# Last stage of a fused attention and mixture-of-experts kernel: the scores' small products in one piece, the sums' small products in one piece, and the transposes of the sums ahead of the mask

## What is computed

```python
h = einsum('bhid,oi,od->bho', x, weighted_sum, weight)        # token mixing, image tokens only
h = concatenate([h, txt], axis=1)
h = h + attention(layernorm(h))      # 16 heads of 16, cosine scores over the 8 batch rows of a token
h = h + ffn(layernorm(h))

def ffn(x):                                                   # the last stage
    q = (rmsnorm(x) @ Wq + bq).reshape(b, t, 16, 16)
    k, v = split(((rmsnorm(x) @ Wdown + bdown) @ Wup + bup).reshape(b, t, 16, 32), 2, axis=-1)
    att = softmax(einsum('bthd,btgd->bthg', q, k) / sqrt(16)) # a token's 16 heads against each other
    x = x + (einsum('bthg,btgd->bthd', att, v).reshape(b, t, 256) @ Wo + bo)
    h2 = rmsnorm(x)
    gate = softmax(h2 @ Wg + bg)                              # 8 experts, all of them used
    return x + einsum('btd,edf,bte->btf', h2, We, gate)
```

## Time and profile before

| what | value |
|---|---|
| median of 3 runs | 841.62 us (840.92 to 843.73) |
| the profiled execution | 842.31 us, span in the profile 840.5 us |
| mean granted TensorE clock | 0.974 |
| PE busy | 777.3 us, 92% |
| PE weight loads busy | 516.1 us, 61% |
| DVE busy | 730.3 us, 87% |
| ACT busy | 335.5 us, 40% |
| POOL busy | 413.3 us, 49% |
| scores' small products (line 868) | 4736 records, 57.2 us |
| sums' small products (line 879) | 4736 records, 56.5 us |

### The profile page before, as it was taken

The page is one execution under the profiler, slowest core; times in us unless marked ns, Lnnn a source line. Parts: engine busy times, 40 slices in busy tenths (PEclk is TensorE's granted clock), DMA queues, the critical chain, the costliest instruction groups (busy, mean ns, idle before and its releaser), DMA issues.

```text
span 840.5 us, 48630 instructions
## 1 busy us (share of the span) xinstructions
PE 777.3 (92%) x20348; PEld 516.1 (61%) x20348; DVE 730.3 (87%) x1702; ACT 335.5 (40%) x874; POOL 413.3 (49%) x1158
## 2 busy tenths in 40 slices
PE   4999978998989899976899999999999999999998
PEld 3888755666666666654556666665666566666654
DVE  5799578899999999964789999999999999999997
ACT  4577333444444444422333333333333333333331
POOL 1331355566666666672445544554455545554321
PEclk9999998999999999975899999999999999999999
DMA  9985000000000000000000000000000000000000
GB/s 328 335 230 190 1 4 4 1 0 0 0 0 0 0 0 0 2 4 3 4 16 16 6 12 12 12 6 12 12 12 12 6 12 12 12 6 13 13 17 20
DMA packets 17062, 28.33 MB, mean 34 GB/s; under 512 B 3475, under 2 KB 12259, under 8 KB 17003
## 3 DMA queue, kind: packets, MB, share of 16 engines
q1 hardware_dynamic: 17002, 27.49, 10.1%
HBM read 22.64 MB, written 4.83 MB: 33 GB/s over the span
## 4 chain that ended last, share of the span: by engine, by line
PE 52%; DVE 1%; issue 1%; ACT 0%; POOL 0%; ACTq 0%
PE bank L197 12%; PE bank L199 10%; PE bank L198 10%; PE bank L868 6%; PE bank L879 6%; PE bank L895 2%; PE bank L933 2%; PE bank L886 2%; PE bank L939 1%; PE bank L919 1%; PE bank L920 1%; DVE sc L1041 0%; DVE smax L1038 0%; DVE acc L1026 0%; DVE res L1026 0%
## 5 line engine op out<-in xcount | busy, mean ns | idle before, releaser
L197 PE MATMUL bank<-we_h,h_t_h 128*128 128x512 f16 x296 | 113.0, 382 | 0.2
L199 PE MATMUL bank<-we_h,h_t_l 128*128 128x512 f16 x296 | 112.2, 379 | 0.0
L198 PE MATMUL bank<-we_l,h_t_h 128*128 128x512 f16 x296 | 112.2, 379 | 0.0
L1026 DVE SCALAR_TENSOR_TENSOR acc<-bank,gate,acc 128x256 f32<-128x256 f32 x222 | 105.4, 475 | 7.0 <-PE bank L199 2.5
L197 PE MATMUL bank<-tokw_h,x_t_h 128*128 128x256 f16 x256 | 70.8, 277 | 11.4 <-DVE x_t_l L643 11.4
L198 PE MATMUL bank<-tokw_l,x_t_h 128*128 128x256 f16 x256 | 70.7, 276 | 0.0
L199 PE MATMUL bank<-tokw_h,x_t_l 128*128 128x256 f16 x256 | 70.7, 276 | 0.0
L879 PEld LDWEIGHTS bank<-pr_t,v 32*32 32x32 f32 x4736 | 48.0, 105 | 33.6 <-issue 33.6
L466 POOL TENSOR_TENSOR rt<-rn 128x32 f32<-128x32 f32 x111 | 26.6, 240 | 80.9 <-DVE rn L441 75.1
L868 PEld LDWEIGHTS bank<-kv_t,fq_t 32*32 32x32 f32 x4736 | 48.8, 107 | 17.7 <-issue 17.7
L879 PE MATMUL bank<-pr_t,v 32*32 32x32 f32 x4736 | 56.5, 194 | 2.7 <-issue 2.6
(11 more groups left out here) (207 smaller groups left out, 2231.0 us busy)
## 6 DMA issues: line engine op xcount, KB each, us to landing
xbuf<-in_x SPq DMA_DIRECT2D x32, 512.0 KB, 5.4
out<-res SPq DMA_DIRECT2D x36, 128.0 KB
we_s<-in_we SPq DMA_DIRECT2D x4, 512.0 KB, 7.0
inw<-in_in_w SPq DMA_DIRECT2D x1, 768.0 KB, 11.3
wrep<-in_w_rep SPq DMA_DIRECT2D x1, 512.0 KB, 4.9
h_all<-in_txt SPq DMA_DIRECT2D x1, 512.0 KB
wst<-in_wst_in SPq DMA_DIRECT2D x1, 256.0 KB, 2.7
outw<-in_out_w SPq DMA_DIRECT2D x1, 256.0 KB, 11.1
```

The costliest lines, as they stand in the source:

```text
L197: nc.tensor.matmul(dst, a_h(c), b_h(c), start=start and c == 0, stop=False)
L198: nc.tensor.matmul(dst, a_h(c), b_l(c), start=False, stop=False)
L199: last = nc.tensor.matmul(dst, a_l(c), b_h(c), start=False, stop=stop and c == chunks - 1)
L1026: op = nc.vector.scalar_tensor_tensor(out=(res if e == E - 1 else acc)[:, :], in0=b_we[s % 2][:, k * D:(k + 1) * D], scalar=gate[p][:, e:e ...
```

## The change

PE's body in the last stage gets another order. No instruction of computation is added or removed, and the programs of the other engines stay as they are.

- The transposes of `on` come first in the body, ahead of the mask.
- The 16 score pieces follow the mask in one go; the semaphore `f_s` is set before the `q` product instead of after it.
- The 16 sum pieces are made in one go before expert step 2; `f_av` is set before expert step 2 instead of after it.

```diff
             def body(i, p):
-                if real(i, 0):
-                    pe.wait_ge(f_qt, i + 1)
-                    nc.tensor.matmul(b_s3[:, :], fm[:, 0:P], fm[:, P:], start=True, stop=True,
-                                     skip_group_check=True)
-                    scores(range(0, 8))
                 if real(i, -1):
                     pe.wait_ge(f_on, i)
                     wait(pe, f_h2l, i - 1)
...
                     last.then_inc(f_onps, 1)
+                if real(i, 0):
+                    pe.wait_ge(f_qt, i + 1)
+                    nc.tensor.matmul(b_s3[:, :], fm[:, 0:P], fm[:, P:], start=True, stop=True,
+                                     skip_group_check=True)
+                    scores(range(0, 16)).then_inc(f_s, 1)
                 if real(i, 1):
                     pe.wait_ge(f_htl, i + 2)
                     wait(pe, f_logit, i - 1)
                     rows_times(b_q[:, 0:D], hn_h, hn_l, lambda c: wq_h[:, c, :],
                                lambda c: wq_l[:, c, :]).then_inc(f_q, 1)
-                if real(i, 0):
-                    scores(range(8, 16)).then_inc(f_s, 1)
                 experts(i, p, 0)
...
                     wait(pe, f_of, i)
-                    sums(range(0, 8), p)
+                    sums(range(0, 16), p).then_inc(f_av, 1)
                 experts(i, p, 2)
-                if real(i, 0):
-                    sums(range(8, 16), p).then_inc(f_av, 1)
                 if real(i, -1):
                     pe.wait_ge(f_x2, i)
```

## The result

The changed kernel takes 865.15 us (median of 4 runs, 864.08 to 866.59), the kernel before on the same chip 842.67 (4 runs, 840.92 to 844.19): ratio 1.027, 95% interval 1.024 to 1.030, slower by 22.5 us. The prediction was 841.9 with a range of 836 to 848. The profiled execution after took 864.84 with a span of 863.1, against 840.5 before.

The account below looks back on a forecast made before the run. A handing back and forth between PE and DVE bounds the kernel; a new loop through `on`, 11.71 + 0.22, keeps the turn at 11.93 us. 34 turns change by 0, the last adds 0.3: 841.9 us, range 836 to 848.

Parts of the forecast that it names:

- The loop through `on`: New loop of waits from expert step 0 over `combine` 2 and `on` to the transposes and `q`: 11.71 + L a turn.
- Start of step 0 to end of step 2: PE's stretch from expert step 0 through the joined sums to the end of expert step 2: 6.79 us.
- The wait of `combine` 2 for step 2: DVE would wait ahead of `combine` 2 for expert step 2, now behind all sums: about 0.15 to 0.2 us.
- L: Wait from the end of `on` to the transposes' start: 0.35 at the loop's top, 0.08 elsewhere, mean 0.22 us.
- The rival of three waits in series: Between the end of `on` and the transposes: L 0.40 at the top, 0.30 elsewhere; turn 12.06, 846.5 us; chance 0.20.
- The joined pieces in the loop: Scores and sums each in one piece of 128 records on PE, 1.21 us to the next start.
- PE's waits: PE idles 0.5 us or more ahead of the gate product and newly ahead of the transposes; busy share about 92%.
- the transposes to the mask: PE's transposes of `on`, now ahead of the mask, put at 0.21 us in each turn.
- `combine` 2 to the end of `on`: DVE's stretch in the loop through `on`, put at 2.48 us a turn.
- The first turns of the stage: Turns at the last stage's start, where PE idles for other engines: nothing, with 1 us of uncertainty either way.
- The clock falls: Rival: PE's granted clock drops to its lower level; a fifth of the turns would cost over 60 us; chance 0.01.
- My own sign of being wrong: A granted clock under 1.00 after 409 us was listed among the signs that would show the forecast wrong.

Follow-up runs that it names:

- the kernel with `q` last: Against the kernel before, the `q` product moved behind both halves of the scores, in the loop's bodies only, nothing joined: 842.87 us, ratio 1.001.
- the version that gains: Against the kernel before, only the scores joined in one piece: 839.39 us, ratio 0.996; with this in the loop's bodies only, 839.11 us, ratio 0.995.

## Why the prediction was wrong

Right, by its own steps:

- *The loop through `on`.* Start of step 0 to end of step 2 was put at 6.79 and is 607.46 - 600.67 = 6.79. The wait of `combine` 2 for step 2 is 0.20, forecast 0.15 to 0.2. Halving the sums took it away, and the turn with it.
- *L.* Forecast 0.35 at the top of the loop and 0.08 elsewhere; it is 610.40 - 610.06 = 0.34 and 624.09 - 624.04 = 0.05. The rival of three waits in series is out, though its sign was right.
- *The joined pieces in the loop.* 1.21 forecast, 1.22 measured, twice.
- *PE's waits.* 0.5 or more ahead of the gate product: 0.56. A new one ahead of the transposes (line 895 before, 890 after): 0.35 at the top. PE's busy share fell to 94% in the 29 turns (334.02 of 355.15), forecast 92%.

Mis-sized: *the transposes to the mask*, put at 0.21, as the pair of 610.64 in the earlier trace rows takes up to the expert step behind it. They take 624.46 - 624.09 = 0.37, and 0.37 at the top of the loop too. This is 0.16 of the 0.21 us by which the turn (mean 12.14) exceeds my 11.93; `combine` 2 to the end of `on` took 2.52 and 2.56 instead of 2.48, the rest. Times 34 it is 7 us, and alone would have given 849, just out of my range. The row that I took showed a pair with an expert step behind it. What makes the pair cost more here is not shown. It isn't only that it has been released by a wait: in the body without the 0.35 of idle time it takes 0.37 as well, and in the kernel with `q` last the same pair, which nothing holds up, takes 0.37 with scores behind it:

```profile
613.98 0.44 PE L897 MATMUL bank<-ident,on 128*128 128x128 f32 x2
614.35 0.75 PE L868 MATMUL bank<-kv_t,fq_t 32*32 32x32 f32 x64
```

Up to the `q` product it takes 0.24 to 0.28, for instance 606.82 - 606.58 = 0.24 with the scores joined. So the cost goes with what follows the pair, and a row with the right successor was needed.

Failed outright, two steps:

- *"The first turns of the stage, where PE idles for other engines, I put at nothing, with 1 us of uncertainty either way."* I worked out one steady turn and multiplied by 34, and took the 1.21 of the earlier trace rows, a lone piece, for what joining costs everywhere. The written-out turns and the first pass of the loop are newly fetched code, where a joined piece costs up to 1.7 more in the kernel after. 6.5 us went there. The clue stood in the trace of before: its gap of 0.52 inside a piece of 64, and above all the 1.89 at 396.83, inside a run of 128 one turn ahead of the row that I took.
- *"The clock falls", at a chance of 0.01.* I compared shares of busy time over long stretches and priced a fall by a fifth of all turns, over 60 us. The falls are short: 3.4 us each, 1.7 lost, four of them. In the loop PE's new wait has a part in them, since four matmuls put into it took them away. 6.8 us in all. My own sign of being wrong, a granted clock under 1.00 after 409 us, came true. The Trainium skill (TensorE: Matmul & The Clock Gate, Part 1), which I had cited against an order that makes PE wait, pointed the right way here; but most turns with the same waits passed without a fall.

The sign could have been had, the size only with these two.

Open: why the clock falls in the written-out turns (it does in the version that gains as well); about 1 of the 22.6 us; and why three kernels that also make PE wait in the loop, the transposes first, the sums joined alone (PE busy 312.8 of 330 us) and both joined (312.5), had no fall between 480 and 800 while after (310.1) had two. One difference stands in the traces. After, and with the change in the loop only, PE waits twice within 1 us at the top of the loop, 0.56 ahead of the gate product and 0.35 ahead of the transposes, and all four falls of these two loops begin 1.5 to 1.7 us behind the mask of such a turn. The sums joined and both joined have only the first wait; the transposes first, and the kernel with four more matmuls, only the second. That fits, and no run tests it.

## What to carry to other kernels

A gain or loss worked out for a steady turn holds for code that the engine has already run; price the written-out turns and a loop's first pass separately, and expect gaps in long runs of very short instructions there. Before calling a loop of waits the limit, look at every wait on it for a second releaser that ends within a tenth of a microsecond: taking the first away wins nothing. And a new wait on PE can have two prices, its length and the clock after it.

## What the runs showed of the hardware

- PE stood still inside runs of small float32 products for up to 2.2 us in new code, with a 16 KB instruction transfer begun 2.3 to 2.7 us before it went on (five gaps after), and never in code that a loop had run once; two bodies of about 12 us each were executed for 330 us without one transfer on q8, the queue of those transfers.
- A fall of the granted clock to 0.50 lasted 3.4 us and cost 1.7, with PE busy 310 of 330 us around it; with four matmuls of 256 columns in the wait of 0.56 the loop had no fall.
- Two float32 transposes took 0.21 up to an expert step and 0.24 to 0.28 up to the `q` product, but 0.37 up to the mask product, and 0.34 to 0.37 up to small products.
